# Edge attributes' products with the low weights: 64 rows of the array each, two feature chunks side by side

## What is computed

```python
src, dst = (edge_index[0], edge_index[1])
edge_feat = jnp.concatenate([x[src], x[dst], edge_attr], axis=-1)
h = mish(edge_feat @ W1 + b1)
messages = mish(h @ W2 + b2)
agg = jax.ops.segment_sum(messages, dst, num_segments=x.shape[0])
```

## Time and profile before

| | |
|---|---|
| median of 3 runs | 1433.16 us (1428.68 to 1433.31) |
| the profiled execution | 1435.59 us, of which 1433.9 us is the span shown |
| PE busy | 1265.1 us, 88% |
| PE weight loads | 1016.0 us, 71% |
| DVE busy | 1026.9 us, 72% |
| ACT busy | 853.3 us, 60% |
| POOL busy | 677.8 us, 47% |
| mean granted TensorE clock | 0.947 of full speed |

### The profile page before, as it was taken

One profiled execution on the slowest core, in us unless ns is written; L12 is line 12 of the kernel. 1 busy time (PEld: TensorE's weight loads), 2 busy tenths in 40 slices (PEclk: granted clock), 3 DMA queues, 4 the chain that ended last, 5 costly groups with the idle time before them and its releaser, 6 DMA issues. The chain is left out here.

```text
span 1433.9 us, 19078 instructions
## 1 busy us (share of the span) xinstructions
PE 1265.1 (88%) x5927; PEld 1016.0 (71%) x5927; DVE 1026.9 (72%) x1798; ACT 853.3 (60%) x762; POOL 677.8 (47%) x473
## 2 busy tenths in 40 slices
PE   2955999999999999999999971797778994998998
PEld 2844778888788888788888851586566883886886
DVE  3222899999999999999999991345853337847345
ACT  1115999999999999999999970345322101321211
POOL 0027778888888888888888511002610001011000
PEclk9986999999999999999999995798989997999999
DMA  5668767777777777777777512876003310000001
GB/s 188 256 228 186 155 142 142 160 153 155 154 154 158 161 158 155 150 151 152 154 152 147 93 20 37 307 259 219 30 30 110 134 31 29 13 4 1 1 8 66
DMA packets 103430, 179.34 MB, mean 125 GB/s; under 512 B 34818, under 2 KB 40112, under 8 KB 103368
## 3 DMA queue, kind: packets, MB, share of 16 engines
q0 software_dynamic: 70032, 104.09, 37.1%
q1 hardware_dynamic: 30848, 69.56, 14.1%
q10 hardware_dynamic: 2488, 4.89, 1.0%
HBM read 138.59 MB, written 37.11 MB: 123 GB/s over the span
## 5 line engine op out<-in xcount | busy, mean ns | idle before, releaser
L476 POOL DMA_INDIRECT G<-q_dram,idx_all x168 | 346.3, 2061 | 54.6 <-issue 45.9
L755 PE MATMUL ps_x<-w_hi,hT_hi 128*128 128x512 f32 x672 | 269.0, 400 | 1.3 <-DVE hT_lo L554 1.3
L755 PE MATMUL ps_x<-w_lo,hT_hi 128*128 128x512 f32 x672 | 262.4, 390 | 0.0
L755 PE MATMUL ps_x<-w_hi,hT_lo 128*128 128x512 f32 x672 | 261.6, 389 | 0.0
L468 POOL DMA_INDIRECT G<-p_dram,idx_all x168 | 173.5, 1033 | 146.6 <-issue 143.4
L755 PEld LDWEIGHTS ps_x<-w_hi,hT_hi 128*128 128x128 f32 x672 | 126.2, 188 | 31.5 <-issue 1.7
L755 PEld LDWEIGHTS ps_x<-w_hi,hT_lo 128*128 128x128 f32 x672 | 126.2, 188 | 27.4
L755 PEld LDWEIGHTS ps_x<-w_lo,hT_hi 128*128 128x128 f32 x672 | 126.2, 188 | 25.2
L717 PE MATMUL ps_x<-ident,G 128*128 128x128 f32 x672 | 103.5, 277 | 30.6 <-DMA G<-q_dram,idx_all 23.0
L561 DVE TENSOR_TENSOR x<-ps_x,b 128x512 f32<-128x512 f32 x168 | 114.9, 684 | 20.1 <-PE ps_x L755 18.1
L717 PEld LDWEIGHTS ps_x<-ident,G 128*128 128x128 f32 x672 | 85.9, 144 | 54.5 <-DMA G<-q_dram,idx_all 23.4
(11 more groups left out here) (252 smaller groups left out, 2859.4 us busy)
## 6 DMA issues: line engine op xcount, KB each, us to landing
ea_raw<-in_eaT SPq DMA_DIRECT2D x84, 128.0 KB, 4.4
adj_dram<-adj_sb POOLq DMA_DIRECT2D x42, 210.2 KB, 4.6
adj_dram<-zeros SPq DMA_DIRECT2D x11, 640.5 KB, 4.2
adj_in<-adj_dram SPq DMA_DIRECT2D x10, 640.0 KB, 4.7
adjT_dram<-adjT_sb SPq DMA_DIRECT2D x10, 640.0 KB, 5.9
adjT_rest<-adjT_dram SPq DMA_DIRECT2D x8, 640.0 KB, 8.9
w_raw_n<-in_w SPq DMA_DIRECT2D x4, 1024.0 KB, 7.8
agg_dram<-agg_sb POOLq DMA_DIRECT2D x42, 84.0 KB, 9.4
```

The source lines that it names most:

```text
L476: g.indirect_dma_start(G[:, b.slot, c * D:(c + 1) * D], None, q_dram, bass.IndirectOffsetOnAxis(ap=idx_all[:, i:i + 1], axis=0), compute_o ...
L755: last = t.matmul(ps_x2[c % 2][:, :], h[:, b.slot, e], w[:, k, :], start=(k == 0 and i == 0), stop=(k == KD - 1 and i == 2))
```

## The change

- `wc_hi` is used as before: one matmul over 128 rows for each chunk, with `ea_parts` (high above, low below).
- `wc_lo` is now multiplied with the high part alone, over 64 rows. For two chunks of a pair the first matmul takes rows 0 to 63 and the second rows 64 to 127 of the weights and of a new tile `ea_high`, which holds the rounded attributes in all 128 partitions. The two matmuls use different rows of the array and write to different PSUM banks. The low·low product is no longer made.
- DVE rounds into `ea_high` (128 partitions), copies the upper 64 partitions once more into `ea_parts`, and subtracts as before: three instructions in place of two.
- `first` is called twice for a block, with a pair of chunks each, and `pre_ready` rises by 2 at the end of a pair. In each pair the waits stand ahead of its first transpose, as before.

```diff
-                        v.tensor_copy(ea_parts[:, b.slot, :], ea_raw[:, b.slot, :]).then_inc(ea_hi, 1)
+                        v.tensor_copy(ea_high[:, b.slot, :], ea_raw[:, b.slot, :]).then_inc(ea_hi, 1)
+                        v.tensor_copy(ea_parts[0:ED, b.slot, :], ea_raw[0:ED, b.slot, :])
                         dve_.wait_ge(ea_hi, b.count(1))
                         v.tensor_tensor(ea_parts[ED:P, b.slot, :], ea_raw[ED:P, b.slot, :],
-                                        ea_parts[ED:P, b.slot, :].bitcast(F32), ALU.subtract).then_inc(ea_ready, 1)
+                                        ea_high[ED:P, b.slot, :].bitcast(F32), ALU.subtract).then_inc(ea_ready, 1)
...
-                        out = ps_x1[:, f * BE:(f + 1) * BE]
-                        for c in range(TE):
-                            t.matmul(out[:, c * P:(c + 1) * P], G[:, b.slot, c * D + f * P:c * D + (f + 1) * P], ident[:, :],
-                                     start=(c == 0), stop=False, is_transpose=True)
-                        for i, w in enumerate((wc_hi, wc_lo)):
-                            last = t.matmul(out, w[:, f * P:(f + 1) * P], ea_parts[:, b.slot, :], start=False, stop=(i == 1))
-                        last.then_inc(pre_ready, 1)
+                        pair = (2 * half, 2 * half + 1)
+                        for f in pair:
+                            for c in range(TE):
+                                t.matmul(ps_x1[:, f * BE + c * P:f * BE + (c + 1) * P], G[:, b.slot, c * D + f * P:c * D + (f + 1) * P],
+                                         ident[:, :], start=(c == 0), stop=False, is_transpose=True)
+                            t.matmul(ps_x1[:, f * BE:(f + 1) * BE], wc_hi[:, f * P:(f + 1) * P], ea_parts[:, b.slot, :],
+                                     start=False, stop=False)
+                        for u, f in enumerate(pair):
+                            rows = slice(u * ED, (u + 1) * ED)
+                            last = t.matmul(ps_x1[:, f * BE:(f + 1) * BE], wc_lo[rows, f * P:(f + 1) * P], ea_high[rows, b.slot, :],
+                                            start=False, stop=True)
+                        last.then_inc(pre_ready, KD // 2)
```

More of the change, by code:

```diff
@@ L394, in edge_phase @@
         ea_parts = sb("ea_parts", [P, 2, BE], F32R, ctx)
+        ea_high = sb("ea_high", [P, 2, BE], F32R, ctx)
         G = sb("G", [P, 2, TE * D], F32, ctx)
@@ L705, in _, with first @@
                 t = nc.tensor
-                def first(b, f):
+                def first(b, half):
                     if b.real():
-                        if f == 0:
+                        if half == 0:
                             pe.wait_ge(ea_ready, b.count(1))
                             pe.wait_ge(q_in[b.slot], b.slot_count(16 * TE))
-                        if f % 2 == 0 and b.at(-1).real():
-                            pe.wait_ge(h1_ready, b.at(-1).count(2, f // 2 + 1))
-                        out = ps_x1[:, f * BE:(f + 1) * BE]
-                        for c in range(TE):
-                            t.matmul(out[:, c * P:(c + 1) * P], G[:, b.slot, c * D + f * P:c * D + (f + 1) * P], ident[:, :],
-                                     start=(c == 0), stop=False, is_transpose=True)
-                        for i, w in enumerate((wc_hi, wc_lo)):
-                            last = t.matmul(out, w[:, f * P:(f + 1) * P], ea_parts[:, b.slot, :], start=False, stop=(i == 1))
-                        last.then_inc(pre_ready, 1)
+                        if b.at(-1).real():
+                            pe.wait_ge(h1_ready, b.at(-1).count(2, half + 1))
+                        pair = (2 * half, 2 * half + 1)
[10 more added lines that the diff above has]
+                        last.then_inc(pre_ready, KD // 2)
                 def adjacency(b):
@@ L759, in step @@
                 def step(s):
-                    for f in range(KD):
-                        first(s.at(1), f)
+                    for half in range(2):
+                        first(s.at(1), half)
                     second(s, 0)
```

## The result

The changed kernel takes 1443.34 us (median of 4 runs, 1442.29 to 1443.76), the kernel before 1432.0 us beside it (4 runs, 1428.68 to 1433.31). The ratio is 1.0077, with a 95% interval of 1.0058 to 1.0095: **slower by 0.8%, about 11 us**. The forecast was 1428.8 us, 0.3% faster. The range of 1424 to 1449 held the time, the sign was wrong, and what came is nearly the mild form of the first rival (1441).

A forecast was written before the change was run, and what follows sets the result against it. Bound: PE's and DVE's full loops, tied at the handover. PE -0.40 and DVE +0.21 us gave a 0.09 us shorter step, 3.4 us over some 38 steps, plus 1 us early: 4.4 off 1433.16, so 1428.8 us; range 1424 to 1449.

The forecast's parts named there:

- the first rival: Edge loop, numbered 1: changing rows costs PE 0.14 (mild, 1441 us) to 0.27 us (1455), four times per step; chance 0.30.
- What bounds the kernel: Edge loop: PE's own 17.14 us and DVE's 16.94 per step, both engines full; the step takes 17.27.
- the tie of both: Handover at step end: late `m_lo` ties the loops; step at least half of (both loops + 0.46 us).
- If the two of a pair run at the same time, 0.46 us saved: PE in `first`: four `wc_lo` matmuls cost 0.92 us per step, 0.46 if pairs overlap; 0.40 saving taken.
- Two loads thus fit under the 0.23 us of the preceding `wc_hi` matmul, if they may run ahead: PE weight loads before a pair: starts 0.11 us apart, hidden under the matmul ahead; a late second leaves 0.38 saved.
- the 42-row matmuls of the earlier trace: Preparation, before the loop: going from 42-row to 128-row matmuls took 0.21 us against 0.07, so 0.14 for a change.
- The harsh price: PE at each row change: waiting until the matmul ahead ended costs 0.27 us each, 1.08 per step.
- The list of signs: Changed trace: pair starts under 0.05 us apart; 0.23 from `wc_hi` to pair if changes are free, 0.37 to 0.50 otherwise.
- The new cast is issued ahead of that wait and fills it: DVE's attribute split: the added cast partly hides in the subtraction's wait for rounding, adding 0.21 us per step.
- Rival 3: DVE's split: the added instruction costs 0.42 us, making DVE's 17.36 the bound, +2.6 us, 1435.8; chance 0.08.
- DVE becomes the bound: Handover in the edge loop: DVE no longer waits at L561; PE waits for `m_lo` in each step instead.
- The tied step: Edge loop: (17.15 + 16.74 + 0.46) / 2 = 17.18 us in place of 17.27, 0.09 less.

The follow-up runs named there:

- DVE's part alone: Kernel before with only DVE's three instructions of the change, PE's low products still over 128 rows: 1441.32 against 1431.85 us, ratio 1.0075.
- PE's: Kernel before with only PE's 64-row pairs, DVE's two instructions kept, output not the reference's: 1437.31 us, ratio 1.0039.
- without overlap: 64-row pairs with DVE as before, but both low products of a pair on rows 0 to 63: 1456.25 us, ratio 1.0167.
- the order alone: Kernel before with a pair's low products behind both high ones, over 128 rows, `pre_ready` by two: 1433.36 us, ratio 1.0011.
- The later subtraction: Changed kernel with DVE's subtraction moved behind the first set of one-hots: 1444.23 against 1434.15 us, ratio 1.0061.
- the four low products in one run: Kernel before with all four low products in one run over 64 rows, DVE's two instructions kept: 1432.88 against 1434.15 us, ratio 0.9993.

## Why the prediction was wrong

- **What bounds the kernel: right.** Two full engines, DVE's loop, PE's loop and the tie of both. With loops measured in the same trace, the largest of the three gives the step within 0.02 us in 12 of the 14 profiles: 17.63 for the changed kernel (17.61 measured), 17.50 for DVE's part alone (17.49), 17.43 for PE's (17.43). The other two each have one long step that the formula doesn't know, of 19.2 and 22.58. Without that frame the result would look like one cost; it is two.
- **"If the two of a pair run at the same time, 0.46 us saved": right** in what it says of the overlap. The two start together, and without overlap the step is 0.43 longer.
- **"Two loads thus fit under the 0.23 us of the preceding `wc_hi` matmul, if they may run ahead": this step failed.** At a change of rows they don't run ahead: the load row is idle for 0.25 us, and load and matmul start together. The sum had nothing for the four changes of a step; they cost 0.75 (0.29 + 0.46), so PE's part came out at +0.29 where -0.40 stood. A price was in the text: 0.14 from the 42-row matmuls of the earlier trace rows, up to 0.27. It measured 0.18 to 0.21. I gave the value zero although the one row near it said 0.14. The value to take was the row's, with the doubt as to the slow start as part of the range. Four times 0.14 would have given the first rival's 1441.
- The Trainium skill, "TensorEngine Tiling (Array Packing)", Key Properties, says that a change of the tiling mode drains the engine. The runs agree, with 0.25 us of idle weight loads at each change and 0.18 to 0.21 us of PE's time. The harsh price that I had worked out for a full drain, 0.27, is too high: its 0.11 from load to matmul came, but the start ahead of it comes 0.31 behind the last matmul, not the 0.39 of that one's row.
- The list of signs took 0.23 for the distance from `wc_hi` to the pair if changes cost nothing. It is 0.32 there, as the order alone shows, and the prediction's own reading was 0.31. So the 0.41 that came is 0.09 of cost, and the rest of the way in shows one start later.
- **DVE's part: this step failed too.** "The new cast is issued ahead of that wait and fills it" gave 0.21; 0.44 came (16.92 to 17.36). 0.32 of it is in the split itself, 0.77 on average in place of 0.45: the new cast holds DVE for its 0.34, and the subtraction still starts 0.43 behind it, where I had 0.33. The later subtraction shows that it keeps such a gap behind an unrelated one-hot too, so it is not a wait for the rounding that a cast could fill. The remaining 0.1 lies in DVE's short instructions, below. Rival 3 had 0.42 as its price.
- **"DVE becomes the bound": wrong.** Both engines got slower, so the tie stayed, and with it DVE's waits for PE at L563.
- The tied step was 17.18 in the sum and is 17.63 with the loops as measured. Of these 0.45 us, 0.35 are half of PE's error (0.69) and 0.11 half of DVE's (0.23), less 0.01 since DVE's loop before is 16.92 on average. Rival 1's 17.46 was nearest, but partly by luck: PE's changes cost 0.13 more per step than its mild price, and DVE's instruction 0.21 more, which makes 0.17 in the tied step; yet its +7.4 us is not far from the 11. The 0.35 us of the steps, over 40 of them, would be 14 us, which is too much: the 37 steps from 179 us on (178 in the changed kernel) add up to 12.5 us more, and the part of the loop ahead of them is 1.0 us shorter, as it is, by 1.1, with the order alone.
- By the steps DVE's part alone costs 0.22 and PE's 0.16, together 0.38, and both together 0.35: PE's 0.29 counts half while the loops are tied. The times of +9.5, +5.5 and +11 us have intervals too wide to show this.

## What to carry to other kernels

Sharing the array between two matmuls of 64 rows pays for its way in and out only if enough pairs stand in one run: here two changes cost 0.35 to 0.43 us and a pair of 512 columns gives 0.23, so one pair loses and two about break even (PE's loop fell by 0.03). Where two engines are both full, size the small instruction that the other one gets before the gain, as it may weigh as much. And look at who hands over to whom at the end of a step: a consumer's input that stands one instruction too late ties two loops together, and a gain on one of them is halved until it is moved.

## What else the runs showed of the hardware

- Two loads of 64 rows, on different rows of the array, run side by side: the row of both lasts 0.19 us, as long as one of 128 rows. On the same rows the two take 0.29 us.
- DVE's short instructions vary in length, and where POOL's gathers start and end goes with it. In the kernel before, a one-hot of L595 lasts 0.40 us, not 0.32, where a gather of POOL ends 0.33 us after its start; all 22 lengthened ones between 400 and 780 us stand like that. In the changed kernel 34 of 252 one-hots hold DVE over 0.03 us longer, by 2.5 us together against 1.6 before. All 34 stand within 0.06 us of the start or end of a gather, where 44% of all one-hots stand. With DVE's part alone, the pair of `m_hi` casts is 0.20 us longer in most steps, which stands next to no start or end of a gather. The rows of the long tensor-tensor instructions stay within 0.07 us in these kernels. No run took this apart, so its cause stays open; it makes up about 0.1 us of a step in the changed kernel, and some 0.2 in the profile of the four low products in one run, where DVE's instructions are those of before.
